# Filler matmuls among TensorE's first and last turns of a four-layer graph network, and new step orders on every engine

## What is computed

```python
# 0: attention with adjacency weights
w = adj * exp(q @ k.T);  a0 = (w / w.sum(2)) @ v
# 1: three graph convolutions
z = relu(adj @ (x @ W1) + b1); z = relu(adj @ (z @ W2) + b2); a1 = adj @ (z @ W3) + b3
# 2: hypergraph convolution up to 512 features, relu, layer norm, back to 256
H = (adj != 0); out = Dn * (H @ (Be * (H.T @ (x @ W.T)))) + b
# 3: eight-head attention, scores multiplied by 2 * adj, softmax, output projection
x = layernorm(x + layer(x, adj))      # after each of the four
```

## Time and profile before

| | us |
|---|---|
| median of 3 runs | 1098.75 |
| lowest and highest run | 1094.12, 1099.09 |
| the profiled execution's own time | 1099.65 |
| its span, first to last instruction | 1097.6 |
| TensorE busy | 1034.2 |
| VectorE, ScalarE, POOL busy | 796.9, 683.3, 481.6 |
| mean granted TensorE clock, share of full | 0.973 |

### The profile page before, as it was taken

One profiled execution on the slowest core, in us unless ns is written; L12 is line 12 of the kernel. 1 busy time (PEld: TensorE's weight loads), 2 busy tenths in 40 slices (PEclk: granted clock), 3 DMA queues, 4 the chain that ended last, 5 costly groups with the idle time before them and its releaser, 6 DMA issues.

```text
span 1097.6 us, 23273 instructions
## 1 busy us (share of the span) xinstructions
PE 1034.2 (94%) x8368; PEld 917.7 (84%) x8368; DVE 796.9 (73%) x2175; ACT 683.3 (62%) x1995; POOL 481.6 (44%) x295
## 2 busy tenths in 40 slices
PE   6789999999999999999999999999999999998755
PEld 5588888888989888898988888898988888886644
DVE  4646868778686868778686877868686877867464
ACT  3245683948577593948668494857659394855524
POOL 1225254644444364634535464434436462441504
PEclk9699999999999999999999999999999999999876
DMA  5101100101011010101001010101001010000000
GB/s 220 49 10 49 39 30 30 59 29 57 0 46 40 29 57 29 57 26 60 0 29 57 29 57 29 57 0 61 25 29 57 29 57 29 11 1 10 21 20 20
DMA packets 15009, 42.41 MB, mean 39 GB/s; under 512 B 1792, under 2 KB 1792, under 8 KB 14848
## 3 DMA queue, kind: packets, MB, share of 16 engines
q1 hardware_dynamic: 14976, 41.97, 11.4%
HBM read 33.57 MB, written 8.39 MB: 38 GB/s over the span
## 4 chain that ended last, share of the span: by engine, by line
PE 86%; ACT 6%; DVE 4%; issue 1%; POOL 1%; DMA 0%; POOLq 0%; SPq 0%; DVEq 0%
PE ps L454 79%; PE ps L763 4%; ACT pr L919 2%; PE ps L704 1%; ACT fT_high L856 1%; ACT ctxT L928 1%; DVE pr L1209 1%; PE ps L634 1%; PE ps L551 1%; DVE st L1032 0%; DVE fT_rest L1112 0%; POOL rstd L1278 0%; DMA pr<-in_weights 0%; POOL pr L1324 0%; DVE x L1048 0%
## 5 line engine op out<-in xcount | busy, mean ns | idle before, releaser
L919 ACT ACTIVATE pr<-pr,mx 128x128 f32<-128x128 f32 x512 | 201.8, 419 | 6.2 <-DVE mx L1214 6.2
L1324 POOL TENSOR_TENSOR pr<-pr,den 128x1024 f32<-128x1024 f32 x64 | 121.7, 1902 | 66.5 <-DVE den L1218 64.9
L1278 POOL TENSOR_TENSOR rstd<-var,neg_half 128x4 f32<-128x4 f32 (+1 forms) x80 | 72.9, 912 | 125.9 <-DVE var L1043 124.2
L1048 DVE TENSOR_SCALAR x<-x,mv,rstd 128x256 f32<-128x256 f32 x256 | 90.2, 418 | 39.3 <-POOL rstd L1278 39.0
L1303 POOL TENSOR_TENSOR x<-x,rows 128x1024 f32<-128x1024 f32 x16 | 38.0, 2374 | 178.1 <-PE ps L454 178.1
L919 ACT ACTIVATION_READ_ACCUMULATOR pr<-pr,mx 128x1 f32 x512 | 111.0, 217 | 0.0
L1313 POOL TENSOR_TENSOR hv<-hv,neg_half 128x2 f32<-128x2 f32 x32 | 22.5, 702 | 178.3 <-DVE hv L1175 178.2
L1032 DVE BATCH_NORM_STATS2 st<-x 128x6 f32<-128x256 f32 x256 | 93.2, 414 | 1.7
L1209 DVE TENSOR_TENSOR pr<-ps,adjB 128x1024 f32<-128x1024 f32 x64 | 75.3, 1219 | 15.7 <-PE ps L454 15.6
L873 ACT COPY s_s<-ps 128x512 f32<-128x512 f32 x32 | 18.8, 588 | 102.5 <-PE ps L454 102.5
L1122 DVE TENSOR_TENSOR ctx_rest<-ps,ctxT 128x512 fp32r<-128x512 f32 x32 | 22.2, 692 | 82.9 <-ACT ctxT L928 82.9
(11 more groups left out here) (190 smaller groups left out, 3231.1 us busy)
## 6 DMA issues: line engine op xcount, KB each, us to landing
xT<-in_xT SPq DMA_DIRECT2D x16, 512.0 KB, 5.3
x<-in_x SPq DMA_DIRECT2D x16, 512.0 KB, 3.4
out_x<-x SPq DMA_DIRECT2D x16, 512.0 KB, 2.8
adjA<-in_adj SPq DMA_DIRECT2D x16, 256.0 KB, 5.4
adjTA<-in_adjT SPq DMA_DIRECT2D x16, 256.0 KB, 2.7
adjB<-in_adj SPq DMA_DIRECT2D x16, 256.0 KB, 3.6
pr<-in_weights SPq DMA_DIRECT2D x2, 512.0 KB, 6.3
qkT<-in_weights SPq DMA_DIRECT2D x1, 1024.0 KB, 12.3
```

What stands on the lines that cost most here:

```text
L919: act.activation(pr[:, b, k, :], pr[:, b, k, :], ACT.Exp, bias=mx[:, b, k:k + 1], accum_out=den[:, b, 0, k:k + 1]).then_inc(exp_ready, 1)
L1048: dve.tensor_scalar(t[:, b, :], t[:, b, :], mv[i][:, b, 0:1], rstd[i][:, b:b + 1], ALU.subtract, ALU.mult).then_inc(ready, 1)
L1278: pool.tensor_tensor(rstd[i][:, bs], var[i][:, bs], neg_half[:, bs], ALU.pow).then_inc(rstd_ready[i], len(pairs))
L1324: pool.tensor_tensor(pr[:, b], pr[:, b], den[:, b, 1, :].unsqueeze(2).broadcast_to([P, HEADS, P]), ALU.mult).then_inc(pr_ready, 1)
```

## The change

On TensorE a step `keep_busy` is added: four 128x512 fp32r matmuls of a constant tile with itself, into bank 7 in the first turns and bank 1 in the last, whose results nobody reads. It stands at ten places, five in the first turn and five in the last ones. VectorE makes its tile `fill` at the start by one more copy, after the first memset. All orders in the three tables are new, that of the loop included. Cut to its core:

```diff
-    "PE": [("set_att", 0), ("set_down", 0), ("att_t", 0), ("set_wo", 0), ("att_t_rest", 0), ("att_v0", 0),
-        ("att_v1", 0), ("att_scores", 0), ("att_turn", 0), ("att_out", 0), ("gram", 0), ("gcn_ax", 0), ("gcn_1", 0),
+    "PE": [("keep_busy2", 0), ("set_att", 0), ("keep_busy0", 0), ("keep_busy4", 0), ("set_wo", 0), ("set_down", 0),
+        ("att_t", 0), ("att_t_rest", 0), ("att_v0", 0), ("att_v1", 0), ("att_scores", 0), ("att_turn", 0),
+        ("att_out", 0), ("gram", 0), ("keep_busy3", 0), ("gcn_ax", 0), ("gcn_1", 0), ("gcn_1_rest", 0),
...
-    "DVE": [("set_rep", 0), ("set_att", 0), ("set_reps", 0), ("rest_Wv0T", 0), ("rest_att", 0), ("set_down", 0),
-        ("rest_W1", 0), ("rest_WupT", 0), ("set_wo", 0), ("rest_W2", 0), ("rest_Wqk3T", 0), ("rest_WdownT", 0),
-        ("rest_WoT", 0), ("att_exp", 0), ("incidence", 0), ("att_out", 0), ("rest_Wv3T", 0), ("rest_W3", 0),
-        ("att_res1", 0), ("x0_means1", 0), ("x0_means0", 0), ("x0_stats", 0), ("degrees", 0), ("x0_norm", 0),
+    "DVE": [("set_rep", 0), ("set_att", 0), ("set_reps", 0), ("rest_att", 0), ("rest_Wv0T", 0), ("set_wo", 0),
+        ("rest_W2", 0), ("rest_WupT", 0), ("set_down", 0), ("incidence", 0), ("rest_W1", 0), ("rest_WdownT", 0),
+        ("att_exp", 0), ("rest_WoT", 0), ("rest_Wqk3T", 0), ("att_out", 0), ("x0_means0", 0), ("rest_Wv3T", 0),
+        ("att_res1", 0), ("x0_means1", 0), ("x0_stats", 0), ("x0_norm", 0), ("degrees", 0), ("gram_scale", 0),
...
-    "ACT": [("high_WoT", 0), ("high_W1", 0), ("x_high", 0), ("high_Wv0T", 0), ("high_att", 0), ("high_W3", 0),
-        ("high_Wv3T", 0), ("high_W2", 0), ("high_WupT", 0), ("high_WdownT", 0), ("att_t", 0), ("att_v0", 0),
+    "ACT": [("high_W1", 0), ("high_att", 0), ("high_W3", 0), ("high_Wv3T", 0), ("high_WoT", 0), ("x_high", 0),
+        ("high_W2", 0), ("high_WupT", 0), ("high_Wv0T", 0), ("high_Wqk3T", 0), ("att_t", 0), ("att_v0", 0),
+        ("att_v1", 0), ("att_off", 0), ("high_WdownT", 0), ("att_exp", 0), ("att_turn", 0), ("x_split", 0),
...
 SCHEDULE
-        ("B", "hyper_up01_rest"), ("B", "hyper_up2"), ("A", "gram"), ("B", "hyper_up3"), ("A", "gcn_ax"),
+        ("B", "hyper_up01_rest"), ("A", "gram"), ("B", "hyper_up2"), ("B", "hyper_up3"), ("A", "gcn_ax"),
...
-        ("C", "mha_turn2"), ("C", "mha_wo0_high"), ("A", "gcn_2s1_high"), ("A", "gcn_2s0_high"), ("C", "mha_wo0"),
-        ("A", "gcn_2s0"), ("A", "gcn_2s1"), ("C", "mha_turn3"), ("A", "gcn_2a"), ("C", "mha_ctx1"),
-        ("B", "hyper_down0_high"), ("C", "mha_wo1_high"), ("C", "mha_wo1"), ("B", "hyper_down0"),
-        ("B", "hyper_down1_high"), ("B", "hyper_down1"), ("A", "gcn_3s1_high"), ("A", "gcn_3s0_high"),
-        ("A", "gcn_3s0"), ("B", "hyper_out"), ("A", "gram_turn"), ("A", "gcn_3s1")],
+        ("C", "mha_turn2"), ("C", "mha_wo0_high"), ("C", "mha_wo0"), ("A", "gcn_2s0_high"), ("A", "gcn_2s1_high"),
+        ("A", "gcn_2s0"), ("C", "mha_turn3"), ("A", "gcn_2s1"), ("A", "gcn_2a"), ("C", "mha_ctx1"),
+        ("B", "hyper_down0_high"), ("C", "mha_wo1_high"), ("C", "mha_wo1"), ("B", "hyper_down1_high"),
+        ("B", "hyper_down0"), ("B", "hyper_down1"), ("A", "gcn_3s0_high"), ("A", "gcn_3s0"), ("B", "hyper_out"),
+        ("A", "gcn_3s1_high"), ("A", "gram_turn"), ("A", "gcn_3s1")],
...
-        ("C", "mha_exp1a"), ("C", "mha_exp2b"), ("B", "up_out0"), ("B", "up_out1"), ("C", "mha_exp2a"),
-        ("B", "up_out2"), ("B", "up_out3"), ("A", "gcn_ax"), ("C", "mha_exp3a"), ("C", "mha_turn1"),
-        ("C", "mha_turn0"), ("C", "mha_exp3b"), ("C", "mha_ctx0"), ("A", "gcn_1"), ("A", "gcn_2s0"),
+        ("C", "mha_exp1a"), ("C", "mha_exp2b"), ("B", "up_out0"), ("B", "up_out1"), ("B", "up_out2"),
+        ("B", "up_out3"), ("C", "mha_exp2a"), ("A", "gcn_ax"), ("C", "mha_turn0"), ("C", "mha_exp3a"),
+        ("C", "mha_turn1"), ("C", "mha_exp3b"), ("C", "mha_ctx0"), ("A", "gcn_1"), ("C", "mha_turn2"),
...
-    "SP": [("B", "gcn_3a1"), ("A", "att_out"), ("C", "mha_scores1"), ("A", "att_scores"), ("A", "att_turn"),
+    "SP": [("B", "gcn_3a1"), ("A", "att_scores"), ("C", "mha_scores1"), ("A", "att_turn"), ("A", "att_out"),
...
 EPILOGUE, TensorE
+        ("keep_busy0", 1), ("gcn_3a0", 1), ("mha_xt", 2), ("gcn_3a1", 1), ("mha_qk01", 2), ("mha_qk01_rest", 2),
+        ("mha_qk2", 2), ("mha_qk3", 2), ("mha_scores0", 2), ("mha_v0", 2), ("keep_busy4", 1), ("mha_scores1", 2),
...
+        ("mha_turn0", 2), ("mha_turn1", 2), ("keep_busy3", 1), ("mha_ctx0", 2), ("mha_wo0_high", 2), ("mha_wo0", 2),
...
+        ("mha_xt", 1), ("keep_busy2", 1), ("mha_qk01", 1), ("mha_qk01_rest", 1), ("mha_qk2", 1), ("mha_qk3", 1),
+        ("mha_scores0", 1), ("mha_scores1", 1), ("mha_v0", 1), ("mha_turn0", 1), ("keep_busy1", 1), ("mha_turn1", 1),
...
 EPILOGUE, ScalarE, the group before the last
-        ("mha_turn0", 2), ("mha_exp3b", 2), ("mha_turn1", 2), ("mha_exp3a", 2), ("mha_ctx0", 2), ("mha_turn2", 2),
+        ("mha_exp2b", 2), ("mha_turn1", 2), ("mha_exp3b", 2), ("mha_exp3a", 2), ("mha_ctx0", 2), ("mha_turn2", 2),
...
+            def keep_busy(g):
+                if first(g):
+                    pe.wait_ge(fill_ready, 1)
+                for _ in range(4):
+                    mm(ps[:, 7 if g < 3 else 1, :], fill[:, 0:P], fill[:])
...
-            dve.memset(ones[:], 1.0)
+            dve.memset(ones[:], 1.0).then_inc(ones_ready, 1)
+            dve.wait_ge(ones_ready, 1)
+            dve.tensor_copy(fill[:].rearrange("p (b n) -> p b n", b=GB), ones[:].unsqueeze(1).broadcast_to([P, GB, P])).then_inc(fill_ready, 1)
...
-            dve.wait_ge(ones_ready, 1)
+            dve.wait_ge(ones_ready, 2)
```

20 lines of the change are left out of this document (9 added, 11 removed), and 235 rows, old and new, of tables (EPILOGUE, PROLOGUE, SCHEDULE).

## The result

The kernel after took 1084.47 us (median of four runs, 1083.20 to 1087.60) beside 1097.4 us for the one before (four runs, 1094.12 to 1099.09): ratio 0.989, interval 0.9856 to 0.9924. The profiled execution took 1085.29 us, with a span of 1083.1 us. I had forecast 1094.8 us and a range of 1088.5 to 1101.5. The kernel gained far more than I said, and none of my cases holds it.

A forecast was written before the change was run, and what follows sets the result against it. TensorE's own work was taken to bound the loop, chains through all engines with TensorE idle or at half clock the ends. First turns -5.4, loop +3.1, last turns -1.6 gave -3.9 us: 1094.8 us, range 1088.5 to 1101.5.

The forecast's parts named there:

- (b): First turn, TensorE: two fillers ahead of `set_wo` raise the clock about 3 us sooner; `att_v0` starts 1.4 us earlier.
- (d): First turns, TensorE: a filler between `gram` and `gcn_ax` brings the clock back before `gcn_1`; -5.4 us altogether by its end.
- (c): First turns, VectorE: with splits moved back, `x0_norm` begins at 39.6 instead of 42.08 us, -2.5 us including the fillers' share.
- (f): Loop, TensorE: `mha_wo0` ahead of `gcn_2s0_high` covers the 0.38 us `z_high` wait; 0.13 us won, a same-sized `fT_rest` wait left.
- (e): Loop, TensorE: two more returns from f32 to fp32r work at 0.09 us each, +0.18 us a pass.
- (g): Loop, ScalarE: `gram` ahead of `hyper_up2` makes `up_out3`, then `ctxT`, `z_high` and `fT_rest` late, +0.2 us a pass.
- rival A: The loop costs nothing: ScalarE keeps its pace and returns vanish in waits; 1089.3 to 1091.7 us in all, chance 0.25.
- (j): Last turns, ahead of `mha_ctx0`: ScalarE's transposed copy goes before `mha_exp3b`, `keep_busy3` fills what is left; -0.6 us.
- (k): Last turns: filler `keep_busy2` ahead of `mha_qk01` costs +1.0 us but brings the clock back sooner; taken as -0.5 us.
- (l): Last turns: filler `keep_busy1` ahead of `mha_turn1` costs +0.65 us, but the clock rises 3 us sooner; -0.7 us.
- (i): Last turns: filler `keep_busy0` ahead of `gcn_3a0` costs +0.2 us; `keep_busy4` ahead of `mha_scores1` is taken as 0.
- C: Rival for the whole kernel: the fillers do not lift the clock and only add work; +4.4 us, 1103.1 us, chance 0.13.

The follow-up runs named there:

- run 23: Not a label but a count: the kernel before, unchanged, run 23 times beside some of the follow-up kernels; median 1094.76 us.
- no_fill: The kernel after without any of its nine filler steps, all orders staying new: 1093.11 us, ratio 0.9982 to the kernel before.
- no_first_fill: The kernel after without the four filler steps of the first turns: 1088.24 us, ratio 0.9937 to the kernel before.
- no_last_fill: The kernel after without the five filler steps of the last turns, orders kept: 1089.26 us, ratio 0.995 to the kernel before.
- loop_pe_only: The kernel after with the old loop orders on VectorE, ScalarE, POOL and SP, only TensorE's new: 1100.33 us (one run), 63.645 us a pass.

## Why the prediction was wrong

**The sum's base.** I set the change against the profiled execution and a median of three. The kernel before has since run 23, 11 and 11 times, with medians near 1094.5 us, at granted clocks of 0.973 to 0.983; its profiled execution (1099.65 us, clock 0.973) was the longest of all. So the trace pair shows 14.5 us of span, and a fair measure of the change is 0.9914, some 9 us (0.9888 to 0.9941, 6 to 12 us). Part of the 17 us half-clock stretch of the earlier trace rows may have been that one execution's: without fillers, though in the new orders, it was 10 us in two other traces. I had the spread (1094.12 to 1099.09) before me and read the trace as typical.

**First turns: right in size, partly for another reason.** -6.0 against -5.4 us. (a) held. (b) held: eight fillers of 0.44 us, then four cold matmuls and sixteen warm ones of 0.22 us, `att_v0` at 24.90 where I said 24.7. My own figures, 1.4 us saved less the 0.2 us that `set_wo` starts late, give 24.9; I had left out the 0.2. My bound of -3 us for all warm should by the same figures have been about -2. (d) held: `gcn_ax` at 41.48 (said 40.9), the clock back before `gcn_1`, whose end came at 48.0 us (said 47.0). (c) was wrong: the new orders without fillers moved `gcn_ax` by 0.4 us, and with them `x0_norm` began at 41.01 us instead of 42.08, where I had said 39.6. Timeline of VectorE in the kernel after:

```profile
29.86 1.23 DVE L1031 TENSOR_TENSOR WdownT_rest<-pr,WdownT_high 128x1032 fp32r<-128x1032 f32 x1 [2.11 <-ACT WdownT_high L953]
31.01 0.89 DVE L1095 TENSOR_TENSOR p<-e,adjA 128x128 f32<-128x128 f32 x4
```

The softmax product `p` now stands behind a split that waits 2.11 us for ScalarE's `WdownT_high`, though VectorE was free for it from 27.7 us on: I had its end right (29.6 us) and had said that nobody asks before 29.8. `p` came 1.1 us sooner (31.01 for 32.08), about what (b) gave, and `x0_norm` followed it at the same distance. The fillers' share is 2.8 us by the medians; the two traces without them (173.9 and 175.4 us to the first store) are 3 us over the mean of those with them (171.5), which says the same, though two of the latter reach 174.2. That the start runs at half clock, whatever the clock row says, is borne out: fillers in front of `set_down` cut it from 5.20 to 3.91 us. (The 0.36 us beside 0.26 by which I had argued this set a distance between starts beside a duration; by starts it is 0.36 against the 0.22 us measured now.) By the Trainium skill's rule (TensorE: Matmul & The Clock Gate, Part 1, that the throttled state is the default and activity lifts it) this was to be expected, and the trace agrees.

**Loop: the mechanism named rightly, its sizes wrong.** (f) is right: the wait for `z_high` goes and one for `fT_rest` comes. The step that failed is the sum "+0.26 us a pass". (e), "2 x 0.09 = +0.18 us", took only the dear side of a return; with two returns out again the work did not fall. (g), "+0.2 us", put a late `up_out3` in full onto a chain in which ScalarE stopped for 0.06 us; moving `gram` back gained nothing. Without both, -0.12 us a pass remains of my own figures, and -0.09 to -0.12 was measured: rival A's loop, a case to which I had given 0.25. I also missed that the order of TensorE and that of VectorE are a pair (`gcn_3s1_high` and `hyper_y1`); with the other engines in their old orders a pass loses 1.2 us.

**Last turns: the terms of the clock were mis-sized.** The failing steps are (j), (k) and (l). I let each filler bring the clock back "3 us sooner" and let half of that count. What it did was to cut stretches of 10 to 14 us to 3 to 7 us, and they held the densest work of these turns. The forecast's terms beside what the stretch with the filler gained, and what the last turns lost when it alone was left out:

| filler | forecast | stretch, two traces | left out alone |
|---|---|---|---|
| (j) `keep_busy3` | -0.6, from ScalarE's order | -2.1 | +3.6 |
| (k) `keep_busy2` | -0.5 | -1.9 | +2.0 |
| (l) `keep_busy1` | -0.7 | -1.5 | +2.2 |

In (j) I saw a filler only as something to fill the gap and gave it no clock at all. (i) said +0.2 us; that stretch gained 1.0. The Trainium skill's rule on transposes (the same page, Part 4: PE-mode transpose, that they do not keep the clock up as other matmuls do) I had turned into "(l) stays +0.65". That was a wrong use of it: the filler between the two blocks of transposes is an ordinary matmul, and with it the transposes behind ran in 1.16 instead of 1.97 us in the kernel after (1.80 to 1.91 in three other traces, where the next row, `mha_ctx0`, was the first warm one, at 1.08). Whether transposes alone would hold the clock up, no run here shows.

**The rivals and the signs.** C said that the fillers do not lift the clock: refuted by `no_fill`, `no_first_fill` and `no_last_fill`. B's wait did not come, since the other engines' orders had been changed with TensorE's; `loop_pe_only` shows what a new wait in the loop costs, 1100 us in all, though it is one for VectorE's `y` and not the one that B named. The sign was right. The range failed because I took independent small errors for each end; all clock terms were low together, and I had never priced a filler that removes a whole stretch.

**What stays open.** Why fillers in the old orders give 4 us by the median and in the new ones 7 to 8. What decides in which execution a filler leaves the row behind it cold. What lengthens TensorE's work by 0.3 us in a pass of `loop_pe_only`. Whether the loop's new hand-over gives the last turns 1 us.

## What to carry to other kernels

Where a chain of engines leaves TensorE waiting 1 to 3 us again and again at the start or the end, price a stretch of half clock as a whole: all matmuls between two gaps at nearly twice their time (here 1.7 us for 0.93), against 1 to 2 us of filler that lies mostly inside a wait. Put the filler into the gap right ahead of the densest work, and stop when TensorE's next row waits for another engine anyway. Read several executions before a trace's half-clock stretch is taken as the kernel's own, and take one engine's order for a change only together with those that feed it.

## What was not expected of the hardware

Between f32 and fp32r matmuls the change of kind is free in sum. Behind eight transposes the first fp32r pair takes 0.09 us more, and the transposes hand over 0.08 us sooner than in front of f32 work (0.80 for 0.88). Behind the eight 128x256 matmuls of `hyper_out` the first fp32r matmul takes 0.19 us more, and they hand over 0.19 us sooner (1.54 for 1.73).

Identical first turns took 170.2 to 174.2 us in different executions, with half-clock stretches of 3.4 us in nine of them and one of 10.4 in the two longest. The loop's pass, at full clock, repeated within 0.03 us.
